# Expert up products in plain fp32 on 64 rows, two side by side, in place of high and low parts on 128 rows

## What is computed

```
layer 0   n   = layernorm(h)                       # 8320 tokens x 64
          g   = softmax over the two best of (n @ Wg.T + bg)
          y_e = relu(n @ W1[e].T + b1[e]) @ W2[e].T + b2[e]      # 64 -> 256 -> 64
          h  += sum_e g_e * y_e
layer 1   n   = rmsnorm(x) * ln2                   # 8320 tokens x 64
          g   = the two best of softmax(n @ router.T), divided by their sum
          y_e = (silu(n @ w1[e].T) * (n @ w3[e].T)) @ w2[e].T     # 64 -> 170 -> 64
          out = h + sum_e g_e * y_e
```

## Time and profile before

| | |
|---|---|
| median of 3 runs | 1184.48 us (1181.44 to 1195.03) |
| the profiled execution, its time | 1186.37 us |
| its span, first to last instruction | 1184.6 us |
| mean granted TensorE clock | 0.945 |
| TensorE matmul busy | 1049.7 us (89%) |
| VectorE busy | 866.7 us (73%) |
| ScalarE busy | 596.8 us (50%) |
| GpSimd busy | 461.6 us (39%) |

### The profile page before, as it was taken

How to read it: one execution, slowest core, us unless ns; L and a number is a source line. 1 busy time by engine, 2 the same in 40 slices (tenths; PEclk the granted TensorE clock), 3 DMA queues, 4 the chain that set the end, 5 groups by cost and what they waited for, 6 DMA issues and landing times. The chain is left out here.

```text
span 1184.6 us, 24247 instructions
## 1 busy us (share of the span) xinstructions
PE 1049.7 (89%) x8559; PEld 770.0 (65%) x8559; DVE 866.7 (73%) x2081; ACT 596.8 (50%) x1289; POOL 461.6 (39%) x618
## 2 busy tenths in 40 slices
PE   6795878579999999994879969986999999999995
PEld 2474856457777777772655547763777777878783
DVE  1596969757777777774868679973688888777874
ACT  1274646555565566552324437763545454545451
POOL 2235302203443444344345387734043433333434
PEclk8797999989999999998889989997999999999998
DMA  8200000000000000000000000000000000000000
GB/s 229 108 1 1 3 2 2 1 1 2 1 2 1 1 1 1 1 1 1 1 1 1 1 1 3 2 2 1 1 6 7 7 6 7 12 7 7 7 7 12
DMA packets 3456, 13.59 MB, mean 11 GB/s; under 512 B 400, under 2 KB 2192, under 8 KB 2960
## 3 DMA queue, kind: packets, MB, share of 16 engines
q1 hardware_dynamic: 3056, 8.00, 2.4%
q0 software_dynamic: 288, 4.11, 0.9%
HBM read 9.98 MB, written 2.13 MB: 10 GB/s over the span
## 5 line engine op out<-in xcount | busy, mean ns | idle before, releaser
L1318 PE MATMUL moe_psU<-moe_nT_parts,moe_w_hi 128*128 128x320 f32 x988 | 324.4, 339 | 2.4 <-DVE moe_hid L1228 1.2
L1318 PE MATMUL moe_psU<-moe_nT_parts,moe_w_lo 128*128 128x320 f32 x988 | 296.4, 310 | 0.0
L1318 PEld LDWEIGHTS moe_psU<-moe_nT_parts,moe_w_hi 128*128 128x128 f32 x988 | 187.9, 190 | 57.2 <-issue 50.1
L1318 PEld LDWEIGHTS moe_psU<-moe_nT_parts,moe_w_lo 128*128 128x128 f32 x988 | 188.3, 191 | 0.0
L1222 DVE TENSOR_TENSOR moe_hid<-moe_psU,moe_silu 128x320 f32<-128x320 f32 x286 | 139.3, 491 | 62.1 <-ACT moe_silu L1086 52.6
L1013 POOL TENSOR_TENSOR moe_sum<-moe_scaled 128x256 f32<-128x256 f32 x130 | 99.1, 763 | 171.1 <-DVE moe_scaled L1212 170.5
L1086 ACT ACTIVATE moe_silu<-moe_psU 128x320 f32<-128x320 f32 x286 | 125.5, 439 | 56.5 <-PE moe_psU L1318 40.0
L1091 ACT ACTIVATE moe_hid<-moe_psU,middle 128x320 f32<-128x320 f32 x260 | 129.4, 528 | 33.4 <-PE moe_psU L1318 31.1
L1228 DVE TENSOR_SCALAR moe_hid<-moe_psU,middle 128x320 f32<-128x320 f32 x156 | 85.7, 550 | 64.9 <-PE moe_psU L1318 64.1
L1329 PE MATMUL moe_psY<-moe_hid,late 128*64 128x320 f32 x832 | 123.4, 439 | 0.9 <-DVE moe_hid L1222 0.9
L1329 PE MATMUL moe_psY<-moe_hid,middle 128*64 128x320 f32 x832 | 123.4, 439 | 0.7 <-ACT moe_hid L1091 0.7
(11 more groups left out here) (301 smaller groups left out, 1893.8 us busy)
## 6 DMA issues: line engine op xcount, KB each, us to landing
images<-in_x SPq DMA_DIRECT2D x8, 576.0 KB, 11.6
late<-in_late POOLq DMA_DIRECT2D x1, 2456.5 KB, 11.9
out_tokens<-h SPq DMA_DIRECT2D x13, 160.0 KB, 1.8
middle<-in_middle POOLq DMA_DIRECT2D x1, 1554.0 KB, 6.8
early<-in_early SPq DMA_DIRECT2D x1, 1043.0 KB, 19.9
early<-in_early SPq DMA_DIRECT2D x1, 80.0 KB, 2.0
```

The lines of the kernel that those rows point to most:

```text
L1318: last = pe.matmul(psum[:, 0:HALF], w[:, col:col + SPLIT], moving, start=(part == 0), stop=(part == 1))
```

## The change

The parts are gone. `nrm_twice` has the normalised tokens twice, side by side: VectorE writes the first copy, ScalarE the second (`second_copy`, at the places at which `high_parts` stood). Turned, `nTr` has the 64 features in rows 0 to 63 and again in rows 64 to 127. A product is one plain fp32 matmul on 64 rows, with the weights straight from the packed constants; two products are issued one behind the other, one in each row half, into two banks. In layer 0 these are units u and u+1 (so `up` is called at even k only, and waits for the eviction of u-4 and of u-3); in layer 1 they are the silu and the gate kind of unit u. Each of the two has its own semaphore increment. `logits` is a plain fp32 matmul on rows 0 to 63 with eight moving columns, and the sum of its parts goes. In layer 1 the factor `ln2` is applied by ScalarE when it copies the turned tokens, and a dummy Silu stands at the beginning. The order of the other work is as before; VectorE's list of steps (`SLOTS`) only loses those that are gone.

```diff
-        w_hi, w_lo = sb("w_hi", [128, NUP], F32R), sb("w_lo", [128, NUP], F32R)
-        w_gate = sb("w_gate", [128, 2 * E], F32R)
-        nTr = [sb(f"nT_parts{k}", [128, TOK], F32R) for k in range(2)]
-        nrm, split = sb("nrm", [B, T, D]), sb("split", [B, T, 128])
+        nTr = [sb(f"nT_twice{k}", [128, TOK]) for k in range(2)]
+        nrm = sb("nrm_twice", [B, T, 2, D])
...
-                scale = late[:, c["ln2"]] if layer == 1 else 1.0
-                begin = 0
-                for end in piece_ends:
-                    cols = slice(up_cols.start + begin, up_cols.start + end)
-                    act.activation(w_hi[:, begin:end], late[:, cols], ACT.Copy, scale=scale).then_inc(w_hi_set, 1)
-                    begin = end
-                act.activation(w_gate[:, 0:E], late[:, gate_cols], ACT.Copy, scale=scale).then_inc(w_hi_set, 1)
-
-                def high_parts(g):
+                def second_copy(g):
                     act.wait_ge(n_set, g + 1)
-                    need(act, T_mm, g * len(TURNS))
-                    act.copy(split[:, :, 0:D].bitcast(F32R), nrm[:, :, :]).then_inc(hi_set, 1)
+                    act.copy(nrm[:, :, 1, :], nrm[:, :, 0, :]).then_inc(twice_set, 1)
...
-                high_parts(0)
+                if layer == 1:
+                    act.activation(sil[0][:, 0:1], late[:, c["ln2"]], ACT.Silu).then_inc(silu_table, 1)
+                    act.wait_ge(silu_table, 1)
+                second_copy(0)
...
-                    need(dve, lo_set, g)
-                    dve.tensor_tensor(nrm[:, :, :], tile, over_width(stats[:, 2, :]), ALU.mult).then_inc(n_set, 1)
-                    yield
-                    dve.wait_ge(n_set, g + 1)
-                    dve.wait_ge(hi_set, g + 1)
-                    dve.tensor_tensor(split[:, :, D:], nrm[:, :, :], split[:, :, 0:D], ALU.subtract).then_inc(lo_set, 1)
+                    need(dve, T_mm, g * len(TURNS))
+                    dve.tensor_tensor(nrm[:, :, 0, :], tile, over_width(stats[:, 2, :]), ALU.mult).then_inc(n_set, 1)
                     yield
...
-                for _ in range(NORM_STEPS + 1):
-                    next(first)
-                begin = 0
-                for n, end in enumerate(piece_ends + [NUP + E]):
-                    dve.wait_ge(w_hi_set, n + 1)
...
                 def transposes(g, part):
...
-                        last = pe.transpose(psM[:, (t - t0) * B:(t - t0 + 1) * B], split[:, t, :], ident)
+                        last = pe.transpose(psM[:, (t - t0) * B:(t - t0 + 1) * B],
+                                            nrm[:, t, :, :].rearrange("b x d -> b (x d)"), ident)
...
                     for t in range(T):
-                        at = LOGITS_AT + t * 2 * E
-                        last = pe.matmul(psM[:, at:at + 2 * E], nTr[slot][:, t * B:(t + 1) * B], w_gate[:, :], start=True, stop=True)
+                        at = LOGITS_AT + t * E
+                        last = pe.matmul(psM[:, at:at + E], nTr[slot][0:D, t * B:(t + 1) * B], late[0:D, gate_cols],
+                                         start=True, stop=True)
...
                     if layer == 0:
                         wait_evicted(pe, g, u - 4)
-                        turns = [(psU[u % 4], 0, up_mm)]
+                        wait_evicted(pe, g, u - 3)
+                        turns = [(psU[u % 4], col_of[0, chunk], up_mm), (psU[(u + 1) % 4], col_of[0, units[u + 1][2]], up_mm)]
                     else:
                         need(pe, hid_act, g * ACT_PER + (u - 1))
...
-                        for part, w in enumerate((w_hi, w_lo)):
-                            last = pe.matmul(psum[:, 0:HALF], w[:, col:col + SPLIT], moving, start=(part == 0), stop=(part == 1))
-                        last.then_inc(done, 1)
...
+                    for x, (psum, col, done) in enumerate(turns):
+                        rows, at = slice(D * x, D * x + D), up_cols.start + col
+                        pe.matmul(psum[:, 0:HALF], late[rows, at:at + SPLIT], nTr[slot][rows, half * HALF:(half + 1) * HALF],
+                                  start=True, stop=True).then_inc(done, 1)
...
                     for p, k, u in places():
-                        up(g, slot, u, not before)
+                        if layer == 1 or k % 2 == 0:
+                            up(g, slot, u)
```

## The result

| | before | after |
|---|---|---|
| median of runs, us | 1184.09 (4 runs, 1181.44 to 1195.03) | 1262.75 (4 runs, 1256.56 to 1269.75) |
| ratio to before, 95% interval | | 1.0647, 1.0556 to 1.0739 |
| profiled execution, us (span) | 1186.37 (1184.6) | 1266.24 (1264.5) |
| layer 0: first to last start of an up product | 243.0 to 541.0 | 247.9 to 587.1 |
| layer 1: the same | 827.3 to 1165.7 | 870.9 to 1245.2 |

A forecast was written before the change was run, and what follows sets the result against it. TensorE was taken to bound the expert blocks; -25.2 products, +50.7 shape changes, +14.3 logits, +22 evictions and -3.4 first tile make +58.4 us on 1184.6, forecast 1243 us, range 1190 to 1280.

The forecast's parts named there:

- Step 1: Up products: a pair in the two row halves costs 0.536 us against 0.587, -25.2 us over 494 pairs.
- rival C: Up products: no weight load in advance within a row half, +105.7 us, 1349 us; chance 0.05.
- D: Up products: the two row halves don't overlap, so 1480 us in all; chance 0.06.
- Step 2: `token_major` and `transposes` between up products: 0.34 us for each change of array shape and back, together +50.7 us.
- B: Array shape: changing between 64 and 128 rows costs nothing, 1192 us; chance 0.10, its faster form 0.05.
- Step 3: Logits: five records become ten, at the pace of loading 128 stationary columns, +14.3 us over 26 tiles.
- Step 4: Evictions in both layers: two banks fill at once and up products wait for them to empty, +22 us.
- Rival E: Evictions: the waits cost double, up to +23 us more, 1266 us; chance 0.12.
- Step 5: First tile of each block: VectorE's weight cutting and a subtraction go, so work starts earlier, -3.4 us.

The follow-up runs named there:

- e3: Changed kernel with both products of a pair in the same row half instead of one in each; 1567.89 us, one run.
- e4: Changed kernel with up products and logits on all 128 rows, the second copy of n written as zeros; 1442.01 us, one run.
- e6: Changed kernel with logits in the one-record fp32r form, n and router weights rounded to it; 1238.58 us, ratio 1.045 to the kernel before.
- e5: Changed kernel with ScalarE's `read_y` in layer 0 one place later, behind the next eviction; 1252.03 us, ratio 1.051 to the kernel before.
- e8: e5 with three of layer 1's five `token_major` moved so fewer runs of three pairs stand unbroken; 1236.18 us, ratio 1.042 to the kernel before.
- e9: e5, e6 and e8 together, plus layer 0's first four `token_major` in twos behind `down`; 1219.46 us, ratio 1.025 to the kernel before.

## Why the prediction was right, and where it was short

| term | predicted, us | by the runs, us | from |
|---|---|---|---|
| 1 products | -25.2 | -24.2 | pace of pairs |
| 2 changes of shape | +50.7 | +50.8 | after, e3 less e4 |
| 3 logits | +14.3 | +14.4 | e6 |
| 4 evictions | +22 | +36.1 | rest of the blocks; e5 and e8 for parts |
| 5 first tile | -3.4 | -4.1 | after |
| unchanged parts | 0 | +6.9 | starts and ends of the blocks |
| sum | +58.4 | +79.9 | spans 1184.6 and 1264.5 |

**What bounds the blocks** was read from the earlier trace rows, and it is what the terms rest on: in the kernel before TensorE stood idle for 1.2 of 292.5 us and 0.35 of 333.8 at a granted clock of 1.00, with VectorE busy for 75 and 80%, so whatever TensorE's order gets longer by is paid in full, and the pace of its records from start to start is what counts. It held: the steps and waits that are priced below are TensorE's, and they are what the blocks grew by.

**Step 1 held.** The two records of a pair start 6 or 7 ns apart and a pair's two steps take 0.538 us, where 0.536 was taken from `down` and the 64-row records. A record of a product that runs alone takes the same 0.27 a step, on 64 rows (e3) and on 128 (e4). Rivals C and D would show 0.75 and 1.07. The gain is 0.049 us a pair.

**Step 2 held within 0.02 us a visit.** A visit of `token_major` in layer 1 of the changed kernel:

```profile
1107.01 0.43 PE L1294 MATMUL moe_psU<-moe_nT_twice,late 64*128 64x320 f32 x2
1107.37 0.66 PE L1316 MATMUL moe_psM<-early,moe_y 128*128 128x128 f32 x4
1107.96 2.14 PE L1294 MATMUL moe_psU<-moe_nT_twice,late 64*128 64x320 f32 x12
1108.33 0.43 PE L1294 MATMUL moe_psU<-moe_nT_twice,late 64*128 64x320 f32 x2
```

(The third row is the wider view of the records of which the fourth names the second step.) From 1107.01 to 1108.33 is 1.32 us; 1.30 was predicted and 0.97 by B. The pieces: 0.36 to the next start is a step of 0.27 and 0.09; `token_major` takes 0.59 to the next up record where it takes 0.44 in e4; and the first step behind takes 0.37, so 0.10 for weights not loaded in advance. e3 less e4 gives the same sum over a tile. So a way out and back costs 0.34 us, also where only the rows change and the columns stay at 128.

What rival C supposed, that within one row half the load for a record waits until the record before it is over, is not borne out: with all up records in one row half (e3) the step is still 0.27 us. A load there starts with the record ahead of the one it serves, as the one of 604.72 does, TensorE's load and then its record:

```profile
604.72 0.19 PEld L1294 LDWEIGHTS moe_psU<-moe_nT_twice,middle 64*128 64x128 f32 x1
604.71 0.43 PE L1294 MATMUL moe_psU<-moe_nT_twice,middle 64*128 64x320 f32 x1
```

The next record starts at 604.98, 0.08 us behind the load's end and well ahead of the modelled end of the record at 604.71, so the load lies within the step.

**Step 3 held**, as e6 shows.

**Step 4 is the term that was mis-sized**, 22 for some 36 us. By the tiles: layer 0 got 3.29 us longer, of which steps 1 to 3 make 2.04 + 0.55 - 0.78 = 1.81. The other 1.48 come on top of one wait of 0.22 in a tile of the kernel before, so the stalls are 1.70 us, where I had 1.09. Layer 1 got 2.80 longer, of which 2.18 + 0.55 - 1.08 = 1.65, so 1.15, where I had 1.04. The single stall that I did work out is there. The first pair of a tile in layer 0, TensorE and then ScalarE:

```profile
508.62 0.81 PE L1294 MATMUL moe_psU<-moe_nT_twice,middle 64*128 64x320 f32 x4
510.10 1.35 PE L1294 MATMUL moe_psU<-moe_nT_twice,middle 64*128 64x320 f32 x8 [0.67 <-ACT moe_hid L1084]
```

```profile
508.74 0.79 ACT L1068 ACTIVATE moe_y<-moe_psY,middle 128x640 f32<-128x640 f32 x1 [1.79 <-PE moe_psY L1305]
509.43 0.94 ACT L1084 ACTIVATE moe_hid<-moe_psU,middle 128x320 f32<-128x320 f32 x2
```

The second step of the pair ahead starts at 509.00 and ends at 509.27, and the next pair waits until 510.10, for the first of ScalarE's two evictions behind `read_y`, which runs from 509.43 to 509.95: 0.83 us and 0.07 for the load, against 0.75 and 0.10 predicted. e5 takes `read_y` out of the way of that eviction, and 0.99 us of the tile go: some 0.4 here, where the next pair then waits, and the rest at the two places of 0.15 and the one of 0.2 below.

What I left out or had too small, in each tile of layer 0:
- `token_major` itself waits for `read_y`. I had followed only the banks of the up products, and not who else reads what `read_y` writes:

```profile
515.30 0.81 PE L1294 MATMUL moe_psU<-moe_nT_twice,middle 64*128 64x320 f32 x4
516.31 0.63 PE L1316 MATMUL moe_psM<-early,moe_y 128*128 128x128 f32 x4 [0.20 <-issue]
```

  From the last up step at 515.68 to `token_major` is 0.63 us instead of 0.36, so 0.27. The wait is shown as issue, but it ends just behind ScalarE's `moe_y`, which runs from 515.41 to 516.20.
- One pair waits some 0.2 us because ScalarE's second copy of the transposed n, which I costed at nothing as an engine with slack, stands in front of the eviction that it needs. The copy doesn't do it alone: in e5 it stands at the same place and the wait is gone, since `read_y` no longer pushes it back. An engine with slack still has an order.
- Behind two `token_major` steps 0.15 each, where I had 0.08 behind three.

Together with the 0.90 at the first pair that is the 1.70.

In layer 1 the wait of the third of three pairs in a row is 0.14 to 0.15 us and 0.10 at three of its four places, as predicted (0.16 and 0.10), 0.19 and 0.07 at the fourth. It looks like this, TensorE's loads and ScalarE:

```profile
1108.80 0.98 ACT L1079 ACTIVATE moe_silu<-moe_psU 128x320 f32<-128x320 f32 x2 [0.76 <-PE moe_psU L1294]
1109.29 0.29 PEld L1294 LDWEIGHTS moe_psU<-moe_nT_twice,late 64*128 64x128 f32 x3 [0.49 <-ACT moe_silu L1079]
```

So the 14 us that term 4 was short are made up like this. The places that I missed or had too small are worth (1.70 - 1.09) x 12 and (1.15 - 1.04) x 12, some 9 us. Some 3 us are the longer stretch at half the clock in the first tiles, which is no eviction at all and only falls into this row of the table because the row is what is left. The last 2 lie in the first tiles as well. I had taken 5 us off for the waits of the kernel before; 0.22 x 12 of them stood in its steady tiles and are gone, the rest stood in its first tiles, where the changed kernel waits too. I didn't follow that further. Rival E, at 1266 us, came closer than my 1243 for the wrong reason: the stalls that I had found weren't twice as long, there were more of them.

**Step 5 held** in its sum, in part for another reason. From the first instruction of the block to the first up product is 7.0 us instead of 8.7 in layer 0 and 6.1 instead of 8.5 in layer 1. The first tile of layer 1, GpSimd, VectorE, ScalarE and TensorE:

```profile
866.11 1.17 POOL L126 TENSOR_TENSOR moe_stats<-moe_stats,minus_half 128x5 f32<-128x5 f32 x1 [2.41 <-DVE moe_stats L1131]
867.32 0.49 DVE L1135 TENSOR_TENSOR moe_nrm_twice<-n_all,moe_stats 128x320 f32<-128x320 f32 x1 [1.29 <-POOL moe_stats L126]
867.91 0.46 ACT L1043 COPY moe_nrm_twice<-moe_nrm_twice 128x320 f32<-128x320 f32 x1 [1.63 <-DVE moe_nrm_twice L1135]
868.42 1.11 PE L1264 MATMUL moe_psM<-early,moe_nrm_twice 128*128 128x128 f32 x4 [7.41 <-ACT moe_nrm_twice L1043]
```

`nrm` now starts 0.04 us behind the deviation, where 1.5 us lay between them. The deviation itself is also quicker, 1.17 instead of 1.87 us.

**The last 6.9 us** of the spans' difference lie where nothing was changed (the first block begins 6.6 later, the tail is 0.4 longer), and no term could have held them. The median is 1.6% above the forecast, and the interval of the ratio, +66 to +88 us, holds the 73 us that the blocks and first tiles alone add up to.

## What to carry to other kernels

Two products side by side in the two row halves are worth what they save only as long as nothing of another shape stands between them: count every such instruction first, at 0.34 us for each way out and back here, and then the gain (0.05 us a pair here). When two banks are filled at the same moment, follow every reader of every bank and every copy that the evicting engine has in its order, also those whose own cost is nothing. And judge terms by the time of a steady tile, since two whole executions differ by some us in parts that no edit has touched, and two blocks by what the clock does in their first tiles. A version whose total comes out as added up can still have the wrong reason beside it, as e9 has in layer 0: split its tile into the terms too.

## What the runs showed of the hardware that I had not expected

- **One row half only: busy, and yet at half the clock.** In e3 TensorE was busy for 99.7 and 100% of the two windows above, at the same step of 0.27 us as in e4, and still the granted clock averaged 0.92 and 0.95 there, falling to 0.50 in single stretches of 3.4 and 6.8 us, while e4, with all 128 rows, stayed at 1.00, though half of its rows hold zeros. The two kernels differ in the rows of the up products (and of the logits), so in these two executions the busy share alone doesn't tell what clock a stretch gets. With both halves at work (after) it was 1.00 from the second tile of each block on.
- **A GpSimd operation that was slow beside some of VectorE's work, and not beside other.** The same operation on 128 x 5 numbers took 1.54 us (from 236.88) and 1.87 (from 820.15) in the first tiles of the kernel before, while VectorE made the weights' low rests from two operands in SBUF (2.49 us from 236.71 and 3.53 from 819.98), and 1.17 in both first tiles after, where VectorE has nothing to do beside it. That VectorE is busy is not enough: in all 24 later tiles of the kernel before it took 1.17 or 1.18 us, with VectorE's evictions, which read PSUM, beside it. That the weights' rests were the cause fits these cases but was not tried by itself.
